# Causal attention layers: row maxima 28 score tiles ahead in place of 32, operand stores ahead of unit 1's loads, and an early exponent on ScalarE

## The reference

```python
q = jnp.einsum('bsd,de->bse', x, wq).reshape(b, s, NUM_HEADS, hd).transpose(2, 0, 1, 3)
...
q = _rope(q, THETA)
k = _rope(k, THETA)
scores = jnp.einsum('hbqd,hbkd->hbqk', q, k) * scale
scores = jnp.where(causal, scores, -jnp.inf)
attn = jax.nn.softmax(scores, axis=-1)
o = jnp.einsum('hbqk,hbkd->hbqd', attn, v)
...
return jnp.einsum('bsd,de->bse', o, wo)
```

## Time and profile before

| | |
|---|---|
| median of 3 runs | 2902.05 us |
| the profiled execution | 2903.42 us |
| its span in the trace | 2901.7 us |
| TensorE busy | 2618.3 us, 90% |
| VectorE busy | 2288.0 us, 79% |
| ScalarE busy | 1871.3 us, 64% |
| GpSimd busy | 531.0 us, 18% |

### The profile page before, as it was taken

How to read it: one execution, slowest core, us unless ns; L and a number is a source line. 1 busy time by engine, 2 the same in 40 slices (tenths; PEclk the granted TensorE clock), 3 DMA queues, 4 the chain that set the end, 5 groups by cost and what they waited for, 6 DMA issues and landing times. The chain is left out here.

```text
span 2901.7 us, 50700 instructions
## 1 busy us (share of the span) xinstructions
PE 2618.3 (90%) x19196; PEld 983.3 (34%) x19244; DVE 2288.0 (79%) x3516; ACT 1871.3 (64%) x3731; POOL 531.0 (18%) x847
## 2 busy tenths in 40 slices
PE   5998899899999999889978999999999789978778
PEld 2436644222222222623322222222227323335336
DVE  5456545799999998577858999999984878855993
ACT  2212322599999999546655999999995566655203
POOL 0000000310011110122313100111102222222771
PEclk9997999699999999989986999999999799989989
DMA  3220121400000000221114000000000311010000
GB/s 120 84 68 1 43 82 56 147 21 20 20 20 21 20 21 26 81 62 53 40 32 141 21 20 21 19 21 20 21 26 14 99 48 50 30 30 30 0 0 16
DMA packets 71996, 120.80 MB, mean 42 GB/s; under 512 B 16905, under 2 KB 44041, under 8 KB 68586
## 3 DMA queue, kind: packets, MB, share of 16 engines
q1 hardware_dynamic: 71754, 117.57, 12.7%
HBM read 94.19 MB, written 23.33 MB: 41 GB/s over the span
## 5 line engine op out<-in xcount | busy, mean ns | idle before, releaser
L1240 ACT ACTIVATE arena<-ps 128x512 f32<-128x512 f32 (+3 forms) x2816 | 1426.8, 571 | 234.2 <-PE ps L1045 168.7
L1367 DVE TENSOR_REDUCE arena<-ps 128x1 f32<-128x1024 f32 x1024 | 1172.3, 1214 | 24.9 <-PE ps L947 23.2
L947 PE MATMUL ps<-arena 61*128 61x512 bf16 (+4 forms) x2816 | 853.7, 381 | 44.7 <-DVE arena L1367 20.3
L1045 PE MATMUL ps<-arena 64*128 64x512 bf16 (+4 forms) x2768 | 826.9, 371 | 60.1 <-ACT arena L1240 32.2
L974 PE MATMUL ps<-arena 128*32 128x256 f32 (+2 forms) x9200 | 807.3, 423 | 0.4 <-POOL arena L1324 0.3
L1369 DVE CUSTOM_DVE_ANT_0 ps<-ps,arena 128x896 f32<-128x896 f32 (+7 forms) x512 | 376.3, 785 | 97.5 <-PE ps L947 93.3
L1045 PEld LDWEIGHTS ps<-arena 64*128 64x128 bf16 (+1 forms) x2816 | 184.9, 95 | 719.1 <-ACT arena L1240 576.2
L974 PEld LDWEIGHTS ps<-arena 128*32 128x32 f32 x9200 | 181.4, 108 | 422.4 <-ACT arena L1240 210.7
L947 PEld LDWEIGHTS ps<-arena 61*128 61x128 bf16 (+1 forms) x2816 | 193.0, 96 | 168.7 <-DVE arena L1367 83.2
L347 PE MATMUL ps<-xnT,moe_up 128*128 128x512 f32 x448 | 215.5, 606 | 0.0
L1293 POOL TENSOR_TENSOR arena<-arena,ones 16x128 bf16<-16x128 f32 x96 | 43.0, 448 | 903.7 <-ACT arena L1225 848.2
(11 more groups left out here) (243 smaller groups left out, 2509.5 us busy)
## 6 DMA issues: line engine op xcount, KB each, us to landing
arena<-m_w SPq DMA_DIRECT2D x40, 256.0 KB, 3.1
arena<-f_q SPq DMA_DIRECT2D x60, 144.0 KB
arena<-f_k SPq DMA_DIRECT2D x180, 48.0 KB
arena<-in_w SPq DMA_DIRECT2D x4, 2048.0 KB
arena<-a_q SPq DMA_DIRECT2D x14, 576.0 KB
arena<-a_k SPq DMA_DIRECT2D x42, 192.0 KB
a_q<-arena SPq DMA_DIRECT2D x44, 96.0 KB, 2.0
a_k<-arena SPq DMA_DIRECT2D x44, 96.0 KB, 2.0
```

The lines of the kernel that those rows point to most:

```text
L947: last = nc.tensor.matmul(at[:, k0 // CHUNK, 0:n], score_rows(Qop[par], j, slice(q0, q0 + P)), score_rows(Kop[par], j, slice(k0, k0 + n)), ...
L1045: nc.tensor.matmul(ps[:, ring_bank(item), off:CHUNK], shifted_rows(Kop[par], j, slice(kb * P, (kb + 1) * P)), shifted_rows(Qop[par], j, sl ...
L1240: nc.scalar.activation(pr[:, (at % 2) * 4 + j, off:CHUNK], ps[:, ring_bank(item), off:CHUNK], ACT.Exp).then_inc(s.ex, 1)
L1367: nc.vector.tensor_reduce(top, src, AXX, ALU.max).then_inc(s.sread, 1)
```

## The change

`EARLY` becomes 28 in causal layers, and both transposes of maxima move to later places. In the prologue chunk 2's operand stores (in full layers also chunk 3's) move ahead of the load of unit 1's operands, and in causal layers chunk 3's stores move between the store and the load of the first maxima. ScalarE computes one exponent of one element per partition before its wait for the stores, into a new tile `spare` of 4 bytes per partition; every tile carved behind it lies 4 bytes further on. The last two edits and the order of stores act on all four layers.

```diff
-            TURN_AT = ((4, 1), (4, 1)) if full else ((0, 3), (1, 1))
-            EARLY = 26 if full else 32
+            TURN_AT = ((4, 1), (4, 1)) if full else ((1, 1), (2, 1))
+            EARLY = 26 if full else 28
...
             mr = c(P)
+            spare = c(1)
...
-                def put_max(u, par, qc):
-
+                def store_max(u, qc):
...
+                def load_max(u, par, qc):
                     sp.wait_ge(max_stored[qc], 16 * (u + 1))
...
+                def put_max(u, par, qc):
+                    store_max(u, qc)
+                    load_max(u, par, qc)
...
                 store_cut(1)
+                store_cut(2)
+                if full:
+                    store_cut(3)
                 sp.wait_ge(s.qst0, N_CUT)
                 sp.wait_ge(s.kst0, N_CUT)
                 sp.wait_ge(s.kneg, 2)
                 load(1, 1)
                 if full:
-                    store_cut(2)
-                    store_cut(3)
                     put_max(0, 0, 0)
                 else:
-                    put_max(0, 0, 0)
-                    store_cut(2)
+                    store_max(0, 0)
                     store_cut(3)
+                    load_max(0, 0, 0)
...
+                nc.scalar.activation(spare, ones[:, 0:1], ACT.Exp)
                 act.wait_ge(s.qst1, N_CUT)
                 act.wait_ge(s.kst1, N_CUT)
```

## The result

The changed kernel takes 2934.77 us (median of 4 runs, 2931.19 to 2939.07), the kernel before on the same chip 2903.24. The ratio is 1.0112 (95% interval 1.0099 to 1.0125), so it is slower by 31.5 us. Predicted were 2921 us (+19.2) with 2897 to 2941 around it. The profiled execution took 2931.67 us, its span is 2929.9 (before 2901.7, and the table ahead).

A forecast was written before the change was run, and what follows sets the result against it. TensorE's order was taken to set the pace inside a unit. Per causal layer 12.6 + 2.3 - 5 = +9.9 us, two layers +19.8, `f1` -0.6, gave +19.2 us: 2921 us, range 2897 to 2941.

The forecast's parts named there:

- +10 to +24: Whole kernel: the forecast's own band of slowdown in us, around +19.2, given a chance of 0.60.
- second rival: Maxima landing later or first half's also late: +2.8 us or more per unit, +30 to +40 in all; chance 0.17.
- prologue, up to the first exponent: Causal layer's start: moved stores let the first exponent come 2.9 to 6.7 us earlier, taken as -5 us per layer.
- last unit up to step 4: Last unit: four score tiles now in step 0 delay the `attend`, shifting the long wait: +2.3 us (1.7 to 3.2).
- A + 5.7: Step 0 of a unit: four widest-tile reductions in a row are handed on 5.7 us after the second transposed tile.
- there at A + 12.1: Second half's maxima reach TensorE 12.1 us after the unit's second transposed tile, 6.4 us behind the transpose.
- Sum per unit: Causal unit: TensorE 3.1 us late, 0.5 more waiting, less 1.4 and 0.37 won back: +1.8 us (+0.9 to +2.8).
- each 128 columns narrower: A unit's other 28 score tiles: each narrower tile saves TensorE 0.05 us, 1.4 us per unit.
- f1: Full layer: the 0.61 us wait of a transposed tile for ScalarE behind its table load goes: -0.6 us (0 to -1.28).
- The unit swallows it: Inside units: step 0's pause replaces TensorE's 2.0 us idle, so units cost nothing more; 2892 to 2896 us; chance 0.15.
- The chain of the maxima is the bound: Inside units: later landings or late first-half maxima, +2.8 us or more per unit; 2932 to 2942 us; chance 0.17.
- The prologue does not do what it says: Prologue: chunk 3's stores and maxima land only near 1260, gain 1 to 3 us per layer; 2926 to 2930 us; chance 0.08.

The follow-up runs named there:

- e6: Changed kernel with the second half's score tiles in descending order of width, so step 0's four are 640 keys wide instead of 1024: 2903.60 us, ratio 1.0006.
- e1: Kernel before with only EARLY and TURN_AT changed as in the changed kernel, old store order and no early exponent: 2947.78 us, ratio 1.0160.
- e7: Changed kernel with the second half's transpose two transposed tiles later, at the end of step 1: 2934.97 us, ratio 1.0113.
- e2: Kernel before with only the new order of the operand stores: 2892.40 us, ratio 0.9958.
- e10: Kernel before plus new stores, early exponent, last unit's sums loads behind its second-half maxima, second half's tiles widest first, EARLY 32: 2873.69 us.
- e9: Kernel before plus new stores and early exponent, six sums loads issued behind the last unit's second-half maxima in causal layers: 2884.44 us, ratio 0.9937.
- e11: Kernel before plus new stores, exponent, later sums loads, widest-first tiles, EARLY 32, last unit's output projections in steps 6 to 11 (causal): 2868.17 us.
- e12: Kernel before with only TURN_AT changed, as in the changed kernel, EARLY still 32: 2903.17 us, ratio 1.0002.
- e8: Kernel before with only the tile of 4 bytes added, no early exponent: 2904.35 us, ratio 0.9991.

## Why the prediction was right, and where it was off

**Right in kind:** slower, by the turn, with the prologue paying part of it back. The size was too small: the measured +31.5 us lie within the range, but outside the forecast's own +10 to +24 and in the +30 to +40 of the second rival, which had a chance of 0.17. The steps of the sum against the trace, per causal layer:

| term | predicted | a1 | a2 |
|---|---|---|---|
| prologue, up to the first exponent | -5 | -4.5 | -4.4 |
| unit 0 | +1.8 | +3.4 | +2.6 |
| units 1 to 6 | +10.8 | +16.5 | +16.8 |
| last unit up to step 4 | +2.3 | +2.9 | +1.9 |
| rest of the layer | 0 | -2.9 | -0.1 |
| sum | +9.9 | +15.4 | +16.9 |

- **What held.** The transpose at "A + 5.7" and the maxima "there at A + 12.1": in unit 2 they stand 6.06 and 12.50 us from the unit's first tile, and A, the second, is some 0.2 behind it; 0.5 us of waiting before step 4 (0.33 to 0.49 where the clock doesn't fall); the first half's maxima just in time; the same long wait in the last unit (7.74 against 8.57 us, in `a2` 5.86 against 8.32), shifted; the first exponent bound by the maxima and not by chunk 3's stores; unit 1's load 1.7 us later, counted from the layer's first operand store, and the maxima's store landing behind it. The gain of the prologue came out near 5 by two things that offset each other. From the first operand store it is 6.1 and 5.4 us, within the 2.9 to 6.7 of the working. That store itself came 1.6 and 1.0 us later after the table, for which the sum had no term.
- **The step that failed** is the size of one term, "Sum per unit: 3.1 + 0.5 - 1.4 - 0.37 = +1.8 us". The mean is +2.74 in `a1` and +2.80 in `a2`, the upper bound I had named. The first four steps aren't what was missed: where the clock stays up they grew by 3.1 to 3.2 us in `a1`, and the terms give 3.1 + 0.5 - 0.6 = 3.0. Two other things make most of the difference. First, "each 128 columns narrower ... so 0.05 each, 1.4 us" was too much. In the last eight steps narrower tiles and the wait of 0.37 should have given 1.2 us; they gave 0.64. The busy time of TensorE in them, before and after:

```profile
1302.41:1323.31 20.90, 19.74 (x127) 6.21 (x131) 16.55 (x35) 14.65 (x34) 4.64 (x9) 1.00 0.16 61
```

```profile
1298.24:1318.50 20.26, 19.41 (x125) 5.88 (x126) 14.21 (x33) 14.61 (x34) 4.41 (x9) 1.00 0.16 63
```

  It fell by 0.33 and not by 0.8. A price from two rows of the same kind was carried over to a place where the tile next to it waits for ScalarE. Steps 7 to 10 have eight narrower tiles, 0.40 us at that price, and got 0.22 shorter (1310.67 to 1320.93 before, 1306.47 to 1316.51 after). The third and fourth transposed tile of step 7, before and after:

```profile
1311.44 0.70 PE L1045 MATMUL ps<-arena 128*128 128x512 bf16 x2
```

```profile
1307.18 0.75 PE L1052 MATMUL ps<-arena 128*128 128x512 bf16 x2
```

  The first score tile of the step is 0.05 shorter, so these two start earlier; the fourth then waits longer for ScalarE, and the pair takes 0.05 more. Only the second score tile's 0.05 is left. e6 shows the same from the other side, with wider tiles for nothing. Second, the clock: in 4 of the 12 units its fall costs 0.5 to 1.8 us more, 0.3 on the mean of a unit. My sum had no term for that. (The wait of 0.37 us, too, stands ahead of the last widest tile alone, two matmuls, and not ahead of two tiles as I had read it.)
- **Unit 0**, taken by the prediction as one more unit, costs 3.4 us in `a1` and 2.6 in `a2`. From the first exponent to unit 1 it takes 33.97 us in `a1`. In e1, with the old prologue, it is 33.30, and in e7, with the new one, 33.21; both are 2.7 to 2.8 over before like any other unit. So the 0.7 us more in the changed kernel aren't the prologue's. Its clock was at the lower level once more there, at 1258.3 to 1261.7, and in `a1` of e7 it wasn't; but in `a2`, where it fell in both kernels, they differ by 0.5 us too. The cause stays open.
- **The rest of `a1`**, -2.9, doesn't come with the new order or prologue: with both, e7 takes 41.41 us there, the kernel before 41.48 and the changed one 38.55. The mean granted clock in it was 0.78 before and 0.90 after, and the last projections took 0.63 us for a pair of L1015 before and 0.39 for L1022 after.
- **f1**: predicted -0.6. From its first operand store to `a1`'s table it takes 681.7 us against 681.4: nothing came, though TensorE no longer waits for ScalarE at that place.
- **The rivals.** "The unit swallows it" is refuted by every unit. "The chain of the maxima is the bound" named the size (2932 to 2942 us, +2.8 per unit) and e7 shows that the chain does bound the first four steps, but not for the reasons it gave: landing times are what they were (2.41 us from load to TensorE against 2.35), and the first half's maxima are never late. It is the reductions at the chain's head. "The prologue does not do what it says" falls with e2 (and its +24 to +28 are +23 to +27 by its own terms). The rule of the Trainium skill that I had weighed (DMA: Bandwidth & Descriptors, Rules for kernel authors) would have had the gain nearer 6 than 5 us. The trace agrees with it. Chunk 3's stores in `a1` are 780 packets of 1024 bytes there: 624 began at 1238.1 to 1242.8 while the load was under way, and 156 only from 1247.9 on, when it ended. The estimate by the rule, three sixteenths, is 146. The last packet ended at 1250.6, just ahead of the maxima, and the gain from the first operand store was 6.1 and 5.4 us.

## What to carry to other kernels

Work that is spread through a pipeline has a place where its results are due: moving the widest pieces next to that place can make the other engine's time for them, back to back, the head of the chain, and no share of busy time shows it. The same work with the narrow pieces last cost a third per unit (e6: 0.9 to 1.0 us against 2.74), and with the widest ones far from the due place it gained (e10). A long wait that is only shifted, or taken away, should be followed to the next thing due behind it before its length is counted as gain (e9, e11).

## What the runs showed of the hardware that I had not expected

- **The clock falls after short waits.** TensorE never stood still longer than 1.1 us at the turn (0.52, 0.58 and 1.00, with work between), and yet its clock fell in 4 of the 12 units of the changed kernel, and in 4 of 12 in e1. In e7, with 0.45 at most at the transpose, 0.85 behind it and the same total, it fell in none, and every unit took 12.6 to 12.8 in its first four steps. Why it fell in these eight units and not in the other sixteen, whose waits were the same up to there, stays open.
- **Layers whose code is the same shift by several us.** At 240 to 270 us, ahead of every changed instruction, the granted clock was 0.54 to 0.56 in the kernel before, e1, e2, e11 and e12, and 0.66 to 0.77 in the other runs, and there `f1`'s first operand store came 5 to 8 us earlier. The tile of 4 bytes is in all of the latter, but also in e11. e8 has only the tile:

> The kernel before with only the tile of 4 bytes (no exponent). The run with the exponent and its tile was 6.1 us faster than before where 3 was expected, and its trace differs already at 240 to 270 us, ahead of every changed instruction, where TensorE's granted clock was 0.77 instead of 0.55; the same holds for the two other runs with exponent and tile. If the shift by 4 bytes does it, this run is 4 to 6 us faster than before and shows 0.66 to 0.77 there; if the exponent does it, or chance, no difference (-1 to +1 us) and 0.55.

  It shows 0.77 there and the first operand store of `f1` 6.9 us earlier, and still its median is that of the kernel before (2904.35 against 2904.22): its causal layers took 4.1 us more, their first exponents 65.3 and 66.1 us after the table, and what follows `a2` 4.8 us more. Neither answer of the expectation holds. What sets the level of the clock at that place stays open; it is the reason why I compare layers and not only medians.
- **A score tile's width can be free.** In steps 4 to 11 twelve tiles, on average 128 columns wider each, cost 0.05 us together (e6 against the changed kernel), though TensorE is recorded busy for 96% of that time.
